# A scan with attention beside it: half of the turned projection a step earlier, the first widening ahead of the plain projection, the second residual behind the cell scan

## The reference

```python
# attention block, on y_in = layernorm(t)
o  = softmax(q k^T / sqrt(32)) v                 # 8 heads of 32
y  = o @ w_out.T + b_out                         # "projection"
x1 = layernorm(y + y_in) * g1 + b1               # first residual
ff = (gelu(y @ w1.T) * (y @ wv.T)) @ w2.T        # "widening" (w1, wv), "narrowing" (w2)
t  = t + layernorm(ff + x1) * g2 + b2            # second residual

# recurrent cell, 256 steps one after the other, on layernorm(t)
i, o = sigmoid(x U + h V);  g = tanh(x U_c + h V_c)
c = h * c + i * g
h = o * tanh(c)
```

## Time and profile before

| | |
|---|---|
| median of 3 runs | 383.69 us (382.93 to 396.51) |
| the profiled execution | 384.46 us, of which the trace spans 382.6 us |
| PE busy | 352.9 us (92%), 5878 matmuls |
| DVE busy | 238.8 us (62%) |
| ACT busy | 224.6 us (59%) |
| GpSimd (POOL) busy | 56.6 us (15%) |
| mean granted TensorE clock | 0.999 |

### The profile page before, as it was taken

How to read it: one execution, slowest core, us unless ns; L and a number is a source line. 1 busy time by engine, 2 the same in 40 slices (tenths; PEclk the granted TensorE clock), 3 DMA queues, 4 the chain that set the end, 5 groups by cost and what they waited for, 6 DMA issues and landing times.

```text
span 382.6 us, 15322 instructions
## 1 busy us (share of the span) xinstructions
PE 352.9 (92%) x5878; PEld 193.0 (50%) x5931; DVE 238.8 (62%) x1230; ACT 224.6 (59%) x1072; POOL 56.6 (15%) x124
## 2 busy tenths in 40 slices
PE   7998999989999999999899999998999999988886
PEld 2566675554564455455545554554455454543332
DVE  3487775646666666666666566656675666664443
ACT  1476764616854775477558655864686478544342
POOL 3101001311211220122012111211121112110000
PEclk9999999999999999999999999999999999999999
DMA  7000000000000000000000000000000000000000
GB/s 230 3 1 4 12 15 17 14 2 3 3 3 2 9 2 4 3 5 4 3 3 7 5 2 6 2 4 3 7 3 4 3 5 5 2 2 6 2 3 6
DMA packets 4807, 3.98 MB, mean 10 GB/s; under 512 B 3837, under 2 KB 4286, under 8 KB 4734
## 3 DMA queue, kind: packets, MB, share of 16 engines
q1 hardware_dynamic: 4432, 2.45, 2.4%
q10 hardware_dynamic: 302, 0.55, 0.5%
HBM read 2.20 MB, written 0.26 MB: 6 GB/s over the span
## 4 chain that ended last, share of the span: by engine, by line
PE 64%; DVE 15%; ACT 12%; issue 7%; DMA 1%; POOL 0%; DVEq 0%; ACTq 0%; POOLq 0%
PE bank L790 18%; PE bank L399 9%; PE bank L570 8%; DVE bank L1340 6%; PE bank L586 5%; DVE H L1350 5%; PE bank L485 5%; ACT bank L975 4%; ACT bank L968 4%; PE bank L473 4%; PE bank L607 4%; ACT E L894 2%; PE bank L687 1%; PE bank L721 1%; PE bank L422 1%
## 5 line engine op out<-in xcount | busy, mean ns | idle before, releaser
L399 PE MATMUL bank<-FB 128*128 128x512 bf16 (+3 forms) x430 | 126.1, 364 | 9.0 <-issue 7.8
L790 PEld LDWEIGHTS bank<-H,VW 64*32 64x32 f32 x3060 | 52.1, 106 | 104.9 <-DVE H L1350 103.1
L968 ACT ACTIVATE bank<-bank 64x8 f32<-64x8 f32 x256 | 37.6, 147 | 87.7 <-PE bank L790 84.8
L790 PE MATMUL bank<-H,VW 64*32 64x4 f32 x3060 | 74.3, 176 | 12.1 <-DVE H L1350 1.9
L1340 DVE TENSOR_TENSOR_SCAN bank<-bank,SU 64x12 f32<-64x12 f32 x256 | 48.5, 190 | 49.8 <-ACT bank L968 47.1
L1350 DVE SCALAR_TENSOR_TENSOR H<-TO,bank 64x4 f32<-64x4 f32 x256 | 40.7, 159 | 44.8 <-ACT bank L975 34.1
L376 POOL TENSOR_SCALAR E<-E,rinv 128x256 f32<-128x256 f32 x62 | 29.8, 482 | 125.8 <-DVE rinv L1138 125.8
L399 PEld LDWEIGHTS bank<-FB 128*128 128x128 bf16 x483 | 37.8, 98 | 20.7 <-issue 3.1
L975 ACT ACTIVATE bank<-bank 64x4 f32<-64x4 f32 x256 | 38.4, 150 | 16.0
L972 ACT ACTIVATE TO<-bank 64x4 f32<-64x4 f32 x256 | 43.8, 171 | 6.2
L1334 DVE SCALAR_TENSOR_TENSOR SU<-H,bank 64x4 f32<-64x4 f32 x256 | 41.3, 161 | 9.1
(11 more groups left out here) (122 smaller groups left out, 310.6 us busy)
## 6 DMA issues: line engine op xcount, KB each, us to landing
AW<-in_attn_w SPq DMA_DIRECT2D x1, 768.5 KB, 7.9
DW<-in_dcn_w SPq DMA_DIRECT2D x1, 288.0 KB, 6.3
X<-in_x_fm SPq DMA_DIRECT2D x1, 256.0 KB, 3.7
X<-in_x_fm ACTq DMA_DIRECT2D x1, 256.0 KB, 6.1
T<-T0T SPq DMA_DIRECT2D x16, 16.0 KB, 1.8
Y<-YT SPq DMA_DIRECT2D x16, 16.0 KB, 1.8
out_dram<-OUT SPq DMA_DIRECT2D x8, 32.0 KB, 1.5
K<-in_consts ACTq DMA_DIRECT2D x1, 181.0 KB, 4.0
```

Source lines behind the costliest of these rows:

```text
L399: nc.tensor.matmul(idle[:, 0:n], FB[:, 0:P], FB[:, 0:n], start=True, stop=True)
L790: mm = nc.tensor.matmul(gate_out(m, gate, r, slice(B * s, B * (s + 1))), VW[0:C, gate, r], H[0:C, (STEPS * m + s - 1) % RING, :], start=Fa ...
L968: nc.scalar.activation(GT[:, :, 1:3].rearrange("p b g -> p g b"), b_cell[m % 2][0:C, 0:2 * P].rearrange("p (g s b) -> p g s b", g=2, b=B)[ ...
```

## The change

For tiles 1 to 7 (tile 0 keeps its order on PE):
- `project_turned(m, 0)` goes from offset 18 to 17.
- `heads_out` for head group 1 is cut in two: images 0 to 2 at offset 17 (96 columns, new semaphore `o_part`), image 3 at offset 19 (32 columns). The last `weigh` (unit 7, offset 18) waits for `o_part`, since it writes into the bank that the copy reads.
- `project(m, 1)` stays at offset 20 but goes behind `widen(m, 0)`.
- the plan: offset 17 is given 430 ns of work, offset 18 stays at 750, offset 19 has 630 in place of 430. By the formula above the fill at offset 17 falls from 1536 to 768 columns, at offset 19 from 768 to 256; 18, 20 and 21 keep theirs (0, 0 and 512).

For all tiles, R2 goes from offset 26 ahead of the scan to offset 25 behind the scan.

```diff
+HEADS_PART = 17
+SUMMED_2 = 25
+NS_HEADS = 200
...
                 if u == B and m >= 1:
                     pe.wait_ge(o_done, HG * m + 1)
+                if u == NU - 1 and m >= 1:
+                    pe.wait_ge(o_part, m)
...
-                    ns += ... NS_PROJECT * (o in (PROJECT, PROJECT + 1)) + NS_PROJECT // 2 * (o == PROJECT + 2)
+                    ns += ... NS_PROJECT * (o in (PROJECT - 1, PROJECT)) + (NS_PROJECT + NS_HEADS) * (o == PROJECT + 1) + NS_PROJECT // 2 * (o == PROJECT + 2)
...
+                    if o == PROJECT - (m > 0):
+                        project_turned(m, 0)
                     if o == PROJECT:
-                        project_turned(m, 0)
                         (project_turned if m == 0 else project)(m, 1 if m == 0 else 0)
                     if o == PROJECT + 1:
                         (project if m == 0 else project_turned)(m, 0 if m == 0 else 1)
-                    if o == PROJECT + 2:
+                    if m == 0 and o == PROJECT + 2:
                         project(m, 1)
                     if o == WIDEN:
                         widen(m, 0)
+                    if m > 0 and o == PROJECT + 2:
+                        project(m, 1)
...
-            def heads_out(m, hg):
-                dve.wait_ge(pv_mm, NU * m + B * (hg + 1))
+            def heads_out(m, hg, images):
+                dve.wait_ge(pv_mm, NU * m + B * hg + images.stop)
                 dve.wait_ge(y_mm, m)
-                nc.vector.tensor_copy(O[:, hg, :, :]..., b_pv[:, P * hg:P * (hg + 1)]...).then_inc(o_done, 1)
+                return nc.vector.tensor_copy(O[:, hg, :, images]..., b_pv[:, P * hg:P * (hg + 1)]...[:, images])
...
-                    if m > 0 and o in HEADS:
-                        heads_out(m, HEADS.index(o))
+                    if m > 0 and o == HEADS[0]:
+                        heads_out(m, 0, slice(0, B)).then_inc(o_done, 1)
+                    if m > 0 and o == HEADS_PART:
+                        heads_out(m, 1, slice(0, B - 1)).then_inc(o_part, 1)
+                    if m > 0 and o == HEADS[1]:
+                        heads_out(m, 1, slice(B - 1, B)).then_inc(o_done, 1)
...
# in beside_gates
-                    if o == NARROWED:
-                        dve.wait_ge(ff_mm, m + 1)
-                        dve.wait_ge(x1_done, m + 1)
-                        nc.vector.scalar_tensor_tensor(out=R2[:], in0=b_t[:, 0:C], scalar=0.5, in1=X1[:], ...)
# in beside_tanh
+                    if o == SUMMED_2:
+                        dve.wait_ge(ff_mm, m + 1)
+                        dve.wait_ge(x1_done, m + 1)
+                        nc.vector.scalar_tensor_tensor(out=R2[:], in0=b_t[:, 0:C], scalar=0.5, in1=X1[:], ...)
```

More of the change, by code:

```diff
@@ L90 @@
 NS_SCORES, NS_TURN, NS_WEIGH, NS_QUERIES = 570, 300, 320, 580
-NS_PROJECT, NS_WIDEN, NS_NARROW, NS_INPUT, NS_PRELOAD, NS_STATES = 430, 545, 420, 140, 600, 210
+NS_HEADS, NS_PROJECT, NS_WIDEN, NS_NARROW, NS_INPUT, NS_PRELOAD, NS_STATES = 200, 430, 545, 420, 140, 600, 210
 K_ID, K_PAIR = 0, P
@@ L237, in hybrid_kernel @@
             "q_mm", "q_done", "s_mm", "s_max", "e_done", "e_inv", "e_norm", "et_mm", "et_sb", "pv_mm", "o_done"))
-        yf_mm, o_early = sem("yf_mm"), sem("o_early")
+        yf_mm, o_early, o_part = sem("yf_mm"), sem("o_early"), sem("o_part")
         y_mm, r_done, ay_done, h_mm, ge_done, ff_done, ff_mm, t_mv, t_rs, t1_done, ln3_done, xt_mm, xt_done = (
@@ L751, in planned @@
                     ns += NS_QUERIES * (o == queries_at(m)) + NS_SCORES * (o in SCORES_AT) + NS_WEIGH * (o in WEIGH_AT)
-                    ns += NS_TURN * (o in TURN_AT) + NS_PROJECT * (o in (PROJECT, PROJECT + 1)) + NS_PROJECT // 2 * (o == PROJECT + 2)
+                    ns += NS_TURN * (o in TURN_AT) + NS_PROJECT * (o in (PROJECT - 1, PROJECT)) + (NS_PROJECT + NS_HEADS) * (o == PROJECT + 1) + NS_PROJECT // 2 * (o == PROJECT + 2)
                     ns += NS_WIDEN * (o in (WIDEN, WIDEN + 1)) + NS_NARROW * (o == NARROW)
@@ L1216, in _ @@
             heads_of(slice(B // 2, B), b_pv_last, NU).then_inc(o_done, HG)
-            def heads_out(m, hg):
-                dve.wait_ge(pv_mm, NU * m + B * (hg + 1))
+            def heads_out(m, hg, images):
+                dve.wait_ge(pv_mm, NU * m + B * hg + images.stop)
                 dve.wait_ge(y_mm, m)
-                nc.vector.tensor_copy(O[:, hg, :, :].rearrange("p t b -> p b t"),
-                                      b_pv[:, P * hg:P * (hg + 1)].rearrange("p (b t) -> p b t", b=B)).then_inc(o_done, 1)
+                return nc.vector.tensor_copy(O[:, hg, :, images].rearrange("p t b -> p b t"),
+                                             b_pv[:, P * hg:P * (hg + 1)].rearrange("p (b t) -> p b t", b=B)[:, images])
             def norm_stats(m, j, src):
@@ L1279, in beside_gates @@
                                                 GE[:].rearrange("p j q -> p (j q)"), ALU.mult).then_inc(ff_done, 1)
-                    if o == NARROWED:
-                        dve.wait_ge(ff_mm, m + 1)
-                        dve.wait_ge(x1_done, m + 1)
-                        nc.vector.scalar_tensor_tensor(out=R2[:], in0=b_t[:, 0:C], scalar=0.5, in1=X1[:],
-                                                       op0=ALU.mult, op1=ALU.add).then_inc(r_done, 1)
                     if o == STATS[1]:
@@ L1311, in beside_tanh @@
                 for m, o in at(g):
+                    if o == SUMMED_2:
+                        dve.wait_ge(ff_mm, m + 1)
+                        dve.wait_ge(x1_done, m + 1)
+                        nc.vector.scalar_tensor_tensor(out=R2[:], in0=b_t[:, 0:C], scalar=0.5, in1=X1[:],
+                                                       op0=ALU.mult, op1=ALU.add).then_inc(r_done, 1)
                     if m > 0 and o in SUM_AT:
```

## The result

The changed kernel takes **403.64 us** (median of 6 runs, 398.92 to 407.43) against 383.39 us before: a ratio of **1.044** (95% interval 1.039 to 1.050). 382.1 us was forecast. The ratio leaves out the runs that took over 1.5% more than the fastest of their kernel, three of these six (405.40 to 407.43) and the 396.51 of before, so the medians themselves are 1.053 apart.

A forecast was written before the change was run, and what follows sets the result against it. The round of gate sums, tanh, scan, tanh and h was taken to bound the kernel. Four long steps, 0.23 us in 7 tiles, gave 1.6 us, from a median of 383.69 to 382.1 us; range 381.2 to 384.1.

The forecast's parts named there:

- The four long steps: Steps at offsets 18 to 19, 20, 21 and 26, too long by 0.07, 0.03, 0.09 and 0.04 us, would become regular.
- Offsets 17 to 19: Moved turned half on time by 0.14 us at 17, split copy delaying no scan, AY starting at +1.11 of step 19.
- Offset 20, the open question: `widen` ahead of `project` at +0.44, erf at +1.2, next gate sums due at +1.35: 0.09 us gained, nothing charged, 0.10 spare.
- the lower bound: Offset 20 on PE with overlapping records: 0.44 + 0.45 + 0.36 = 1.25 us, before the gate sums due at 1.35.
- The new wait: Last `weigh` at offset 18 waits for the copy part of 17: 0.8 us of slack, cost nothing.
- the residual: R2 behind the scan of offset 25: between nothing and 0.01 us late there, 0.04 us gained at 26.
- It can't be more: Whole change: at most 0.23 us a tile, 7 x 0.23 = 1.6 us, since the round itself is untouched.
- a few single steps that share no offset: Exceptions among the other offsets from 0 to 31, which were otherwise put at 1.14 us.
- the clock: Rival: clock falls in steps 18 to 20, up to 0.29 us a step; 388.2 us if all 21 steps; chance 0.03.
- Step 18 already ran without fill: Argument against the clock falling in steps 18 to 20: step 18 had no fill before the change.
- PE is busier than in most steps: Argument at offset 20 against the clock rule: PE is busy there and nothing was taken from it.
- Mean clock 0.999: Argument against the clock falling in steps 18 to 20: the mean clock before the change was 0.999.

The follow-up runs named there:

- the kernel with 384 and 384 columns: Changed kernel with 384 columns of fill put back at offset 18 and 384 at offset 19 behind the turned projection: 382.78 us, ratio 0.999.
- the fill alone: Kernel before with the changed kernel's fill plan (768 columns at offset 17, 256 at 19), no work moved: 396.58 us.
- the moves alone: Changed kernel with the plan of the kernel before (1536 columns at offset 17, 768 at 19), all moves kept: 388.95 us, ratio 1.012.
- 384 columns back at 18: Changed kernel with 384 columns of fill put back at offset 18 only, none added at 19: 384.68 us, ratio 1.004.
- both gaps filled: Changed kernel with 384 columns put back at offset 19 and 512 or 384 at offset 18: 382.37 us (0.998) or 382.78 us (0.999).
- the residual's first run: First run of the kernel before with only R2 moved behind the scan of offset 25: 393.78 us; ten later runs had a median of 383.11 us.

## Why the prediction was wrong

- **The four long steps, 0.23 us a tile: right.** In the tiles with the clock at 1.00 all four are gone, 7 x 0.24 us in the kernel with 384 and 384 columns.
- **Offsets 17 to 19: right.** The half at 17 starts 0.87 behind h and makes nothing late; the 32-column copy lasts 0.22 (0.21 taken); AY starts 1.13 behind h (1.11 forecast).
- **Offset 20, the open question: right, but by less than was summed.** `widen` starts 0.44 behind h, the gelu's erf 1.19 (1.2), and the gate sums are on time at +0.21. `project` starts 0.55 behind `widen` (271.24 to 271.79), where the lower bound took 0.45; with the 0.36 of that sum it ends at 1.35, just when the gate sums are due. The 0.10 to spare was not there: that nothing was late is partly luck.
- **The new wait and the residual: right.** The wait on `o_part` costs nothing; R2 behind the scan of 25 makes neither 25 nor 26 late.
- **"It can't be more" than 1.6 us held, but the sum was short of a term.** 0.9 comes back as late steps, since the added copies on DVE move its instructions against the places at 64 modulo 128. Steps of that kind were in the trace before ("a few single steps that share no offset") and got no term.
- **The step that failed: the sum has no term for the 1280 columns of fill that were taken, and the rival that stood for them, the clock, got a chance of 0.03.** The runs showed 61.4 us of the scan at 0.50 and 21.2 us for them, more than ten times what the moves won. It was the right mechanism at the right place, and the argument against it was wrong twice. "Step 18 already ran without fill": true, but it ran without a gap too, with `weigh`, two projections and 0.07 of overrun. The change took the turned half out of it and put nothing in. That steps 17 and 19 lost their fill, 18 its work, all beside each other, was not added up (PE's 0.30 us without work became 0.53); only step 20 was looked at ("PE is busier than in most steps"), and the clock fell there, behind the thinned steps. "Mean clock 0.999" is the clock of the profiled run; one of the three runs of before had taken 396.51 us, and no term was made of it. Its clock is not on record; of 35 later runs of that kernel the three at 394 to 400 us were at 0.93 to 0.95. The page of the Trainium skill that was cited ("TensorE: Matmul & The Clock Gate", Part 1: The HAM clock gate) pointed the right way: PE's activity keeps the clock up. The runs agree with it: the changed kernel, the fill alone and the moves alone fell near offset 20 in their traces, with 384 columns back at 18 one tile did, and with both gaps filled none.
- **The price of the rival was mis-sized.** 0.29 us a step at half clock was taken, at 21 steps. Measured: 0.09 for the round alone, and 0.57 with 1536 columns of fill, in 41 steps of the profiled run, since a stretch there lasts 6.8 or 13.65 us once it has begun. The queue behind the gate sums was left out of that price: in the step of the earlier trace rows it is done at +1.26, 0.09 before the next gate sums are due, and the step of 1.71 us above shows how far past them it runs at half clock.

What stays open: what it is in PE's work over these steps that decides; why the clock falls in tile 1 and not in tile 2 of one run; what happens at the 64 modulo 128 places; and the occasional long stretch at 0.5 at the start of the scan.

## What to carry to other kernels

Where an otherwise idle PE is kept busy only to hold its clock, that fill is a resource with a limit: before taking columns or matmuls out of neighbouring steps, add up what PE loses over all of them, and put fill back into each gap that a move leaves (896 columns in two gaps turned 1.044 into 0.998, and 768 did as well, 0.999). Price the fall by the whole PE queue at half rate, the fill included, not by the critical matmuls alone. And where one run in three is 3% longer, look at its granted clock before counting on the others.

## What was not expected of the hardware

- A stretch at the 1.2 GHz level lasted up to 13.65 us in the changed kernel though PE was busy for 12.98 us of it, and in the residual's first run 37.5 us with PE busy for 36.2. Once down, a full queue did not bring the clock back at once.
- DVE has places, 63 to 65 modulo 128 in its instruction count in these traces, at which an h starts up to 0.23 us late (0.28 once). Seven more copies in the scan, or four memsets ahead of it, decide which h it is.
- PE busy by the records was 92% of the span both before and after: the busy share of the whole span told nothing of the fall. Over steps 17 to 20 alone, before any fall, it shows: 4.36 of 4.66 us before, 4.02 of 4.55 after.
